# Order of the convolution's matmuls: by column shift instead of in two phases

## The chip, the cores and the metric

The kernel runs on one core of one Trainium2 chip. The metric is the device time of one execution in microseconds (us); the time of a kernel is the median over its runs. The core has five engines: TensorE (PE, the matmuls; its weight loads are shown apart as PEld), VectorE (DVE), ScalarE (ACT), GpSimd (POOL) and SyncE (SP, which here issues all the DMAs). They wait for one another by semaphores.

## The reference

A vision tower over 128 images of 64x64 pixels. It has a first part, the tokenizer, and seven transformer and expert stages behind it. Only the tokenizer is touched. It embeds each pixel in 32 channels and puts it through four layers, each of which adds a spectral branch and a 3x3 convolution:

```
for i in range(nl):                                   # nl = 4, 32 channels
    h_ft = jnp.fft.rfft2(h)
    w_c = spec_wr[i] + 1j * spec_wi[i]
    out_modes = jnp.einsum('bixy,ioxy->boxy', h_ft[:, :, :mx, :my], w_c)
    spec = jnp.fft.irfft2(out_modes, s=(H, W))
    conv = lax.conv_general_dilated(h, conv_w[i], (1, 1), 'SAME', dimension_numbers=dn)
    conv = conv + conv_b[i][None, :, None, None]
    h = leaky(spec + conv)
```

## The kernel before

Everything is float32. The images are handled in 64 pairs. A pair fills the 128 partitions of a tile `rows_in` as four sections of 32 channels: image a (0 or 1) times s, where s says whether the row of pixels is even or odd. A section holds 32 rows of 64 columns, 2048 pixels, which are cut into four parts p of 512 pixels.

The convolution of the first layer works on the three input channels (`pe_x_conv`, L587) and is not touched. In the other three layers (the loop over `l`, 1 and 2, called mid, and the last one) each pair runs `pe_conv`, so it runs 3 x 64 = 192 times. Its result lies in four PSUM banks, `zbank` 0 to 3, bank 2a + s for image a and output rows of parity s, and part p in the 32 partitions from 32p. A 3x3 convolution needs for each output row its own row and the two beside it, at three column shifts dx:

- an output row of either parity takes two of its three rows from one row index of the input: an even row of the pair and the odd row beside it. Both stand in 64 partitions, so that one matmul with 64 rows and 32 columns of the array does both ("same-row taps", L612). The array holds eight such tiles at a time: two images a by four parts p. There are 3 dx x 2 parities x 8 = 48 such matmuls.
- the third row comes from the row index above or below, in 32 partitions ("neighbour-row taps", L619). The array holds sixteen such 32x32 tiles: 4 sections by 4 parts. There are 3 x 16 = 48 of these.

The profile shows each of these matmuls as two records, the second half of the float32 product behind the first. I call the records of one set of tiles that run at the same time a pass: 8 records for same-row taps, 16 for neighbour-row taps. Before, a pair has 12 passes of the first sort (phase one), then 6 of the second (phase two).

The program of TensorE for pair n is written out in `pe_pair`: `pe_conv` of pair n; then, for the pair before, the transposes `pe_flip` (L631) and the forward transform `pe_forward` (L648), and between them the inverse transform `pe_inverse` of the next pair (L568). At the end of the convolution the semaphore `z_done` lets VectorE add bias and spectral part (L966) and apply the leaky slope (L973); SyncE loads the rows of a later pair behind it (L351). In the last layer the flips and forward transforms are replaced by two small products `pe_q1` (L677) and `pe_q2` (L688).

Inside `pe_conv` there is one semaphore wait that matters here: `gb`, where `pe_forward` collects its result, is `zbank` 3. ScalarE copies it out (`modes_copy`, L841) and then raises `g_ready`. Output rows of odd parity (`so == 1`) go to banks 1 and 3, so TensorE waits for `g_ready` before the first of them in the mid layers.

The loop of a mid layer has two pairs in its body (`over_layer`, L204).

Of the kernel before, what the change touches and what calls it, by code (L numbers as in the profile page):

```python
# [28 lines left out]
ET = 2 + XT  # L29
# [35 lines left out]
def build_tokenizer(nc, x_pairs, grid_rows, embed_w, embed_b, spec_uv, conv_w, conv_b, q1_w, q1_b, q2_w, q2_b,  # L65
                    fwd_dram, inv_dram, sign_dram, eye_dram, tok, h_dram, g_dram, m_dram):

    with ExitStack() as ctx:
# [95 lines left out]
        g_ready = sem("g_ready")  # L164
# [25 lines left out]
        def pe_need(pe, signal, value):  # L190

            if not (isinstance(value, int) and value <= 0):
                pe.wait_ge(signal, value)
                pe.nop(nofuse=True)
# [396 lines left out]
        def pe_conv(pe, u, i, kind, l):  # L591

            n = 2 * i + u + PAIRS * l
            pe_need(pe, z_free, 2 * n)
            pe.wait_ge(rows_loaded[u], 32 * (i + NP * (l - 1) + 1))
            pe.nop(nofuse=True)
            SHIFTED = ((1, slice(0, COLS), slice(0, COLS)), (0, slice(1, COLS), slice(0, COLS - 1)),
                       (2, slice(0, COLS - 1), slice(1, COLS)))

            def moving(part, p, down, cols):  # L600
                start = COLS * (1 + down)
                return rows_in[u][part, start:start + PIX].rearrange("c (h q j w) -> c q h j w", h=2, q=4, w=COLS)[:, p, :, :, cols]

            for so in range(2):
                if so == 1 and kind != "last":
                    pe.wait_ge(g_ready, ET + n - 1)
                    pe.nop(nofuse=True)
                for dx, out, src in SHIFTED:
                    for p in range(4):
                        for a in range(2):  # L610
                            part = slice(64 * a, 64 * a + 64)
                            nc.tensor.matmul(section(zb[32 * p:32 * p + 32, 2 * a + so, :])[:, :, :, out],  # L612
                                             conv_t[part, dx, so, :], moving(part, p, 0, src), start=(dx == 1), stop=False)
            for dx, out, src in SHIFTED:
                for p in range(4):
                    for a in range(2):
                        for s in range(2):
                            part = slice(32 * (2 * a + s), 32 * (2 * a + s) + 32)
                            last = nc.tensor.matmul(section(zb[32 * p:32 * p + 32, 2 * a + 1 - s, :])[:, :, :, out],  # L619
                                                    conv_t[part, dx, 2, :], moving(part, p, -1 if s else 1, src),  # L620
                                                    start=False, stop=(dx == 2))
            last.then_inc(z_done, 1)
# [68 lines left out]
        def pe_pair(pe, u, i, kind, l):  # L691
# [10 lines left out]
            if kind == "first":  # L702
                pe_x_conv(pe, u, i, l)
            else:
                pe_conv(pe, u, i, kind, l)
# [619 lines left out]
class Signals:  # L1325
# [13 lines left out]
    def sem(self, stage, who):  # L1339
        return self.sems[stage, who]  # L1340
# [1638 lines left out]
```

## Time and profile before

| | |
|---|---|
| median of 3 runs | 8086.82 us (8085.25 to 8110.36) |
| the profiled execution | 8098.54 us, span 8096.7 us |
| mean granted TensorE clock | 0.924 |
| busy share of the span | PE 84%, PEld 50%, DVE 61%, ACT 28%, POOL 1% |
| L612 matmul records | 18432, 1151.4 us busy |
| L619 matmul records | 18432, 653.8 us busy |

The span runs from the first to the last instruction of the profiled execution. A busy share is an average over stages with different limits. The ends of matmul records are modelled, so a row's start is better evidence than its end. A granted clock of 1.00 is TensorE's higher level of 2.4 GHz, 0.5 is 1.2 GHz.

### The profile page before, as it was taken

The numbers are of one execution on the slowest core, as the hardware profiler recorded it, in microseconds if no ns is written. First come the engines' busy times: TensorE is split into PE (matmuls) and PEld (weight loads), VectorE is DVE, ScalarE is ACT, GpSimd is POOL, SyncE is SP. The second block draws the span as 40 slices with busy tenths as digits, with TensorE's granted clock in tenths as the row PEclk, the third lists the DMA queues.
The fourth block names the chain that finished last, engine by engine and source line by source line (L and its number), as shares of the span: only waits on it lengthen the run. The fifth ranks groups of instructions, "written<-read, shape, count | busy, mean of one in ns | idle before, by whom it ended". The sixth has DMA issues, their size and how long they took to land. (4 is left out here: it accounts for less than half of the span.)

```text
span 8096.7 us, 285876 instructions
## 1 busy us (share of the span) xinstructions
PE 6837.6 (84%) x120694; PEld 4060.7 (50%) x120694; DVE 4950.5 (61%) x7875; ACT 2232.6 (28%) x3074; POOL 63.0 (1%) x46
## 2 busy tenths in 40 slices
PE   4699986989889699989878999966888888888888
PEld 3566665555555555555554444433344444444443
DVE  2599993666666376666636777756455454454554
ACT  1133321222222122222212222223333333333333
POOL 1000000000000000000000000000000000000000
PEclk7799997999999799999979999978999999999999
DMA  6677775444444544444452222220000000000000
GB/s 182 136 134 135 137 141 147 115 116 115 117 116 114 153 120 116 116 117 115 114 158 69 72 72 72 72 67 3 1 3 3 1 3 3 1 3 3 1 3 2
DMA packets 714748, 641.00 MB, mean 79 GB/s; under 512 B 334881, under 2 KB 583841, under 8 KB 705831
## 3 DMA queue, kind: packets, MB, share of 16 engines
q1 hardware_dynamic: 713800, 626.58, 31.8%
q8 instruction: 814, 13.34, 0.7%
q14 instruction: 134, 1.09, 0.0%
HBM read 353.72 MB, written 285.56 MB: 79 GB/s over the span
## 5 line engine op out<-in xcount | busy, mean ns | idle before, releaser
L612 PE MATMUL zbank<-rows_in,conv_taps 64*32 64x512 f32 (+1 forms) x18432 | 1151.4, 642 | 239.5 <-issue 239.5
L966 DVE SCALAR_TENSOR_TENSOR rows_out<-zbank,conv_bias,work 128x1024 f32<-128x1024 f32 x512 | 633.8, 1279 | 1159.8 <-PE zbank L619 1143.5
L568 PE MATMUL abank<-inv_basis,mode_tile 128*32 128x128 f32 x32768 | 1014.8, 276 | 91.6 <-DMA mode_tile<-m_img 54.9
L834 ACT ACTIVATE turned<-tbank 128x1024 f32<-128x1024 f32 x400 | 410.1, 1025 | 2260.3 <-PE tbank L631 2260.3
L568 PEld LDWEIGHTS abank<-inv_basis,mode_tile 128*32 128x32 f32 x32768 | 884.6, 111 | 255.2 <-issue 254.8
L648 PE MATMUL zbank<-fwd_basis,turned 128*32 128x128 f32 x24576 | 756.1, 274 | 106.2 <-DVE rows_out L966 68.7
L612 PEld LDWEIGHTS zbank<-rows_in,conv_taps 64*32 64x32 f32 x18432 | 381.6, 114 | 919.6 <-issue 905.2
L648 PEld LDWEIGHTS zbank<-fwd_basis,turned 128*32 128x32 f32 x24576 | 682.6, 111 | 128.6 <-issue 127.4
L619 PE MATMUL zbank<-rows_in,conv_taps 32*32 32x512 f32 (+1 forms) x18432 | 653.8, 595 | 6.1 <-issue 6.1
L973 DVE SCALAR_TENSOR_TENSOR rows_out<-rows_out 128x1024 f32<-128x1024 f32 x512 | 601.7, 1217 | 0.0
L1559 PE MATMUL banks<-constants 128*128 128x512 f32 x1040 | 520.8, 654 | 22.4 <-issue 22.4
L988 DVE TENSOR_TENSOR folded<-by_row 128x1024 f32<-128x1024 f32 x400 | 471.3, 1218 | 46.0 <-PE tbank L631 45.6
L619 PEld LDWEIGHTS zbank<-rows_in,conv_taps 32*32 32x32 f32 x18432 | 279.4, 103 | 365.3 <-issue 317.5
L631 PE MATMUL tbank<-eye,folded 128*128 128x128 f32 x3200 | 439.7, 281 | 23.4 <-DVE folded L988 23.4
L631 PEld LDWEIGHTS tbank<-eye,folded 128*128 128x128 f32 x3200 | 346.1, 141 | 220.7 <-issue 220.7
L942 DVE TENSOR_TENSOR work<-spectra 128x512 f32<-128x512 f32 x512 | 330.5, 687 | 78.1 <-ACT spectra L828 78.0
L942 DVE TENSOR_TENSOR work<-inv_copy 128x512 f32<-128x512 f32 x512 | 329.2, 684 | 69.3 <-ACT inv_copy L828 69.3
L828 ACT ACTIVATE inv_copy<-abank 128x1024 f32<-128x1024 f32 x256 | 262.2, 1024 | 342.5 <-PE abank L568 342.5
L1559 PEld LDWEIGHTS banks<-constants 128*128 128x128 f32 x1040 | 211.6, 212 | 262.0 <-issue 259.8
L828 ACT ACTIVATE spectra<-abank 128x1024 f32<-128x1024 f32 x256 | 262.5, 1025 | 260.5 <-PE abank L568 260.5
L1559 PE MATMUL banks<-xT_stacked,weights 64*128 64x512 f32 (+1 forms) x896 | 288.2, 681 | 44.3 <-ACT xT_stacked L1524 31.2
L951 DVE TENSOR_TENSOR work<-work 128x1024 f32<-128x1024 f32 x256 | 312.2, 1219 | 2.3
(356 smaller groups left out, 7672.5 us busy)
## 6 DMA issues: line engine op xcount, KB each, us to landing
h_rows<-rows_out SPq DMA_DIRECT2D x768, 256.0 KB, 3.8
rows_in<-h_rows SPq DMA_DIRECT2D x384, 512.0 KB, 4.9
m_img<-rows_out SPq DMA_DIRECT2D x32, 1024.0 KB, 5.4
mode_tile<-m_img SPq DMA_DIRECT2D x512, 64.0 KB, 3.0
g_half<-modes_out SPq DMA_DIRECT2D x384, 64.0 KB
spectra<-g_half SPq DMA_DIRECT2D x12, 1856.0 KB, 27.3
rows_in<-x_slots SPq DMA_DIRECT2D x96, 194.9 KB
rows_out<-x_slots SPq DMA_DIRECT2D x96, 194.9 KB
```

Of the source, the lines that this page charges most:

```text
L568: last = nc.tensor.matmul(ab[32 * p:32 * p + 32, s, 128 * k:128 * k + 128], mode_tile[u][:, k, a, :], inv[:, k, s, 128 * p:128 * p + 128], ...
L612: nc.tensor.matmul(section(zb[32 * p:32 * p + 32, 2 * a + so, :])[:, :, :, out], conv_t[part, dx, so, :], moving(part, p, 0, src), start=( ...
L619: last = nc.tensor.matmul(section(zb[32 * p:32 * p + 32, 2 * a + 1 - s, :])[:, :, :, out], conv_t[part, dx, 2, :], moving(part, p, -1 if s ...
L631: last = nc.tensor.transpose(tb[:, x, 128 * b:128 * b + 128], folded[:, q, x, b, :], eye[:])
L648: last = nc.tensor.matmul(by_mode(gb[at:at + 32, 0:256])[:, :, :, q, :], turned[q][:, x, 2 * a + s, 32 * p:32 * p + 32], fwd[:, p, 2 * x + ...
L828: nc.scalar.activation(inv_copy[a], ab[:], ACT.Identity).then_inc(a_copied, 1)
L834: nc.scalar.activation(turned[q][:].rearrange("p x b n -> p x (b n)"), tb[:], ACT.Identity)\
L942: last = nc.vector.tensor_tensor(inverse[:, :, 2 * a:2 * a + 2, h, :].rearrange("p y s m -> p s y m"), up, low, op)
L966: nc.vector.scalar_tensor_tensor(out=rows_out[u][:, half].rearrange("p (s x) -> p s x", s=2), in0=zb[:, 2 * a:2 * a + 2, :], scalar=conv_b ...
L973: nc.vector.scalar_tensor_tensor(out=out, in0=out, scalar=0.01, in1=out, op0=ALU.mult, op1=ALU.max)\
L988: nc.vector.tensor_tensor(folded[:, y, :, :, :].rearrange("p x b (j w) -> p (x b j) w", w=COLS // 2), v[:, :, 0, :], v[:, :, 1, :], op).th ...
L1559: return nc.tensor.matmul(out, lhsT, rhs, start=start, stop=stop)
```

## The change

`pe_conv` issues the same 96 matmuls with the same operands, in another order. Before: all same-row taps (parity 0 with its three shifts, then parity 1), then all neighbour-row taps. After: for each shift dx the 8 same-row matmuls of parity 0, the 8 of parity 1, then the 16 neighbour-row matmuls. The wait for `g_ready` stays ahead of the first matmul of parity 1, which now has 8 matmuls ahead of it instead of 24.

```diff
-            for so in range(2):
-                if so == 1 and kind != "last":
-                    pe.wait_ge(g_ready, ET + n - 1)
-                    pe.nop(nofuse=True)
-                for dx, out, src in SHIFTED:
+            for dx, out, src in SHIFTED:
+                for so in range(2):
+                    if so == 1 and dx == 1 and kind != "last":
+                        pe.wait_ge(g_ready, ET + n - 1)
+                        pe.nop(nofuse=True)
                     for p in range(4):
                         for a in range(2):
                             part = slice(64 * a, 64 * a + 64)
                             nc.tensor.matmul(section(zb[32 * p:32 * p + 32, 2 * a + so, :])[:, :, :, out],
                                              conv_t[part, dx, so, :], moving(part, p, 0, src), start=(dx == 1), stop=False)
-            for dx, out, src in SHIFTED:
                 for p in range(4):
                     for a in range(2):
                         for s in range(2):
```

The new file is a line shorter, so L619 of before is L618 of after, and what follows moves by one line too. On TensorE, in the loop body of a mid layer, the convolution of the first of the two pairs stood like this before; a row gives line, operation, output, inputs, output shape and how many alike follow one another, and 32x512 is the unshifted tap, 32x8x63 the two shifted ones:

```order
L595 ISA [waits z_added]
L612 MATMUL zbank<-rows_in,conv_taps 32x512 [waits rows_loaded0]
L612 MATMUL zbank<-rows_in,conv_taps 32x512 x7
L612 MATMUL zbank<-rows_in,conv_taps 32x8x63 x16
L606 REGISTER_ALU
L612 MATMUL zbank<-rows_in,conv_taps 32x512 [waits g_ready]
L612 MATMUL zbank<-rows_in,conv_taps 32x512 x7
L612 MATMUL zbank<-rows_in,conv_taps 32x8x63 x16
L619 MATMUL zbank<-rows_in,conv_taps 32x512 x16
L619 MATMUL zbank<-rows_in,conv_taps 32x8x63 x32
```

The same place of the same engine after the change:

```order
L595 ISA [waits z_added]
L612 MATMUL zbank<-rows_in,conv_taps 32x512 [waits rows_loaded0]
L612 MATMUL zbank<-rows_in,conv_taps 32x512 x7
L607 REGISTER_ALU
L612 MATMUL zbank<-rows_in,conv_taps 32x512 [waits g_ready]
L612 MATMUL zbank<-rows_in,conv_taps 32x512 x7
L618 MATMUL zbank<-rows_in,conv_taps 32x512 x16
L612 MATMUL zbank<-rows_in,conv_taps 32x8x63 x16
L618 MATMUL zbank<-rows_in,conv_taps 32x8x63 x16
L612 MATMUL zbank<-rows_in,conv_taps 32x8x63 x16
L618 MATMUL zbank<-rows_in,conv_taps 32x8x63 x16
```

The array changes between 64x32 and 32x32 tiles five times in a pair instead of once, and the wait for `g_ready` stands 16 matmuls earlier. In the loop body of the last layer, which has no such wait, the same engine stood before like this, behind the product L677 of the pair before:

```order
L612 MATMUL zbank<-rows_in,conv_taps 32x8x63 x16
L612 MATMUL zbank<-rows_in,conv_taps 32x512 x8
L612 MATMUL zbank<-rows_in,conv_taps 32x8x63 x16
L619 MATMUL zbank<-rows_in,conv_taps 32x512 x16
L619 MATMUL zbank<-rows_in,conv_taps 32x8x63 x32
```

And after:

```order
L612 MATMUL zbank<-rows_in,conv_taps 32x512 x15
L618 MATMUL zbank<-rows_in,conv_taps 32x512 x16
L612 MATMUL zbank<-rows_in,conv_taps 32x8x63 x16
L618 MATMUL zbank<-rows_in,conv_taps 32x8x63 x16
L612 MATMUL zbank<-rows_in,conv_taps 32x8x63 x16
L618 MATMUL zbank<-rows_in,conv_taps 32x8x63 x16
```

Here too only the order moved: 48 matmuls of each sort stand in either list. No other engine's program changes.

## Rows read from the trace of the kernel before

**Rows 1.** The page: busy time by engine, and its two groups for the convolution.

```profile
PE 6837.6 (84%) x120694; PEld 4060.7 (50%) x120694; DVE 4950.5 (61%) x7875; ACT 2232.6 (28%) x3074; POOL 63.0 (1%) x46
...
L612 PE MATMUL zbank<-rows_in,conv_taps 64*32 64x512 f32 (+1 forms) x18432 | 1151.4, 642 | 239.5 <-issue 239.5
...
L619 PE MATMUL zbank<-rows_in,conv_taps 32*32 32x512 f32 (+1 forms) x18432 | 653.8, 595 | 6.1 <-issue 6.1
```

**Rows 2.** TensorE's waits in layer 2 (2801 to 4090 us), and line 204's branches.

```profile
PE zbank L612 <- issue: 114.3, 29, 4.8
...
L204 PEldq COMPARE_BRANCH  x90: 76/3504/4955, 352.1 to 4086.7; - x90
```

**Rows 3.** The timeline in layer 1, TensorE's rows: start, length, instructions.

```profile
2517.19 1.09 PE L631 MATMUL tbank<-eye,folded 128*128 128x128 f32 x8
...
2526.50 5.33 PE L612 MATMUL zbank<-rows_in,conv_taps 64*32 64x512 f32 x96
...
2531.76 3.38 PE L619 MATMUL zbank<-rows_in,conv_taps 32*32 32x512 f32 x96
...
2535.07 1.09 PE L631 MATMUL tbank<-eye,folded 128*128 128x128 f32 x8
```

**Rows 4.** Windows: length, busy PE, PEld, DVE, ACT, POOL, clock, DMA.

```profile
2526.50:2531.76 5.26, 5.26 (x101) 1.72 (x97) 5.26 (x6) 0.38 (x1) 0.00 (x0) 1.00 0.44 99
2531.76:2535.07 3.31, 3.31 (x105) 1.45 (x97) 0.02 (x1) 0.00 (x0) 0.00 (x0) 1.00 0.93 205
...
2505.69:2513.88 8.19, 8.19 (x96) 2.99 (x96) 1.13 (x1) 0.00 (x0) 0.00 (x0) 0.64 0.63 141
```

**Rows 5.** Timeline, four narrow windows around changes of the tile size.

```profile
2526.17 0.40 PE L648 MATMUL zbank<-fwd_basis,turned 128*32 128x128 f32 x8
2526.50 0.66 PE L612 MATMUL zbank<-rows_in,conv_taps 64*32 64x512 f32 x8
...
2531.20 0.63 PE L612 MATMUL zbank<-rows_in,conv_taps 64*32 64x504 f32 x8
2531.76 0.77 PE L619 MATMUL zbank<-rows_in,conv_taps 32*32 32x512 f32 x16
...
2534.42 0.71 PE L619 MATMUL zbank<-rows_in,conv_taps 32*32 32x504 f32 x9
2535.07 0.33 PE L631 MATMUL tbank<-eye,folded 128*128 128x128 f32 x1
...
4817.55 0.66 PE L677 MATMUL tbank<-rows_out,q_taps 32*32 32x512 f32 x8
4818.15 0.66 PE L612 MATMUL zbank<-rows_in,conv_taps 64*32 64x512 f32 x8
```

**Rows 6.** Timeline, narrow windows: pairs of same-row passes, by their first record.

```profile
2526.95 1.06 PE L612 MATMUL zbank<-rows_in,conv_taps 64*32 64x512 f32 x16
...
2527.38 1.05 PE L612 MATMUL zbank<-rows_in,conv_taps 64*32 64x504 f32 x16
```

**Rows 7.** Timeline, narrow windows in phase two: neighbour-row passes, by their first record.

```profile
2531.76 1.20 PE L619 MATMUL zbank<-rows_in,conv_taps 32*32 32x512 f32 x32
...
2532.21 1.01 PE L619 MATMUL zbank<-rows_in,conv_taps 32*32 32x512 f32 x17
...
2532.83 1.26 PE L619 MATMUL zbank<-rows_in,conv_taps 32*32 32x504 f32 x32
```

**Rows 8.** The timeline, layer 1: the copy behind `g_ready` and the store it releases.

```profile
2526.79 0.38 ACT L841 ACTIVATE modes_out<-zbank 128x256 f32<-128x256 f32 x1 [0.87 <-PE zbank L648]
...
2527.35 0.62 SPq L382 DMA_DIRECT2D g_half<-modes_out  x1
```

**Rows 9.** The timeline in the last layer: from one convolution to the next.

```profile
4826.82 2.48 DVE L966 SCALAR_TENSOR_TENSOR rows_out<-zbank,conv_bias,work 128x1024 f32<-128x1024 f32 x2 [5.04 <-PE zbank L619]
...
4832.69 1.28 DVE L1037 SCALAR_TENSOR_TENSOR turned<-tbank,q_bias,by_row 128x1024 f32<-128x1024 f32 x1
...
4834.11 1.09 PE L677 MATMUL tbank<-rows_out,q_taps 32*32 32x512 f32 x16 [1.34 <-DVE turned L1037]
```

## The prediction

> **What bounds the kernel now.** I read the page's busy shares first: TensorE leads with 84%, and the two groups of the convolution hold 1151.4 and 653.8 us of it [rows 1]. A share does not say that the engine is the limit where the change sits, so I asked who TensorE waits for in a mid layer. In the whole of layer 2 its one wait of size is ahead of L612, 29 times and 114.3 us in all, for nothing that the profile shows [rows 2]. It comes at the back edge of the loop: the branch of line 204 on TensorE's queue has a median of 3504 ns [rows 2]. It comes once in two pairs, and the order of the matmuls does not touch it. Everywhere else in the mid layers TensorE runs without a pause: the period of an undisturbed pair is 2535.07 - 2517.19 = 17.88 us [rows 3], and each engine that waits there waits for it. So in the mid layers a microsecond more in `pe_conv` is a microsecond more of time.
>
> In the last layer TensorE does wait, 1.34 us a pair, for VectorE's L1037 [rows 9]. That is no slack for the convolution: VectorE's chain starts with L966, which itself waits 5.04 us for the end of the convolution, and runs through L1037 to the product L677, behind which the next convolution starts [rows 9]. The convolution and that chain lie end to end, and here too its length counts in full.
>
> What is left is how long one convolution takes: 5.26 us for phase one and 3.31 us for phase two, 8.57 us, at a clock of 1.00 [rows 4].
>
> **What passes and switches cost.** The work of a pass never changes, only what lies between passes. A same-row pass follows the one before after 0.43 us (2526.95 to 2527.38) [rows 6], and the first one behind a change of tile size after 0.45 (2526.50 to 2526.95) [rows 5, 6]. A neighbour-row pass behind the first takes as long, 0.45 (2531.76 to 2532.21) [rows 7].
>
> A change of tile size is dearer. Four of them are in the rows, from 128x32, 64x32, 32x32 to 128x128 and 32x32 to 64x32. In each the new size's first record starts 0.06 to 0.07 us before the modelled end of the old size's last record: 2526.57 against 2526.50, 2531.83 against 2531.76, 2535.13 against 2535.07, 4818.21 against 4818.15 [rows 5]. Within one size the next pass starts on the first tile while the last ones still run; across a change it waits for the last tile. So a switch costs the stagger of the old pass and about 0.1 us:
>
> - behind a same-row pass (8 tiles): 2531.76 - 2531.20 = 0.56 us instead of 0.43 [rows 5]
> - behind a neighbour-row pass (16 tiles, further apart): the second pass ends at 2531.76 + 1.20 = 2532.96, so the new size would start at 2532.89, 0.68 us behind 2532.21 [rows 7].
>
> The order before pays something too. Phase two changes its shift twice without changing its tile size. There the 17th record of the row that starts at 2532.21 is alone, and the pass proper starts at 2532.83: 0.62 us instead of 0.43, so 0.19 us are lost at each of the two places [rows 7]. The last pass of phase two is staggered more as well: the three pieces 0.45 + 0.62 + 0.45 + 0.62 + 0.44 leave 0.73 of the 3.31 us for it, where I take 0.68 after the change.
>
> **The sum.** One shift after the change: four same-row passes, 0.45 + 0.43 + 0.42 + 0.56 = 1.86 us, and two neighbour-row passes, 0.45 + 0.68 = 1.13 us; together 2.99. Three shifts are 8.97 us, against 8.57: **+0.40 us** a pair. By parts it is four more switches (two at 0.13, two at 0.25, each with some 0.03 of restart, together 0.88 us) less two lost starts in phase two (0.4) and a shorter last stagger (0.05), which gives 0.43. I take 0.40. It comes 192 times: **+77 us**.
>
> The wait for `g_ready`: it stood behind six passes, and now stands behind two, 0.45 + 0.43 = 0.88 us behind the start, at 2527.38 in the pair of the rows. ScalarE's copy ends at 2526.79 + 0.38 = 2527.17, and the store that waits for the same semaphore is issued at 2527.35, 0.18 us behind the copy's end [rows 8]. TensorE needs its weight load on top of that. So the wait is hidden, or up to 0.1 us late, in the one pair of two that does not follow the branch; behind the branch the copy is long done. Behind the waiting instruction the whole rest of the convolution is queued, and VectorE waits for that. 62 pairs by 0.05 are 3 us. Bounds: nothing, or 0.4 us (the copy itself) in each of 128 mid pairs, 51 us.
>
> Pairs behind the branch start at the lower clock: their phase one takes 8.19 us at a mean clock of 0.64 [rows 4]. I add nothing for them. The time at the lower clock is set by what came before it, and a microsecond that a switch wastes there holds only half as many passes; a switch itself may be dearer. I allow 0 to 0.3 us for these 62 pairs, 0 to 19 us, in the range.
>
> The profiled execution is 8098.54 us, so it would become 8098.5 + 77 + 3 = 8179 us. It stands 12 us above the median of 8086.8, which I carry over: **8167 us**, 1.0% slower.
>
> On the switch the Trainium skill has a rule: "TensorEngine Tiling (Array Packing)", section "Key Properties", says that changing the tiling mode drains the engine. The rows agree, with 0.13 and 0.25 us for a drain. "TensorE: Matmul & The Clock Gate", section "Single matmul latency", puts the fixed part of one matmul that overlaps nothing at 398 cycles of 2.4 GHz, 166 ns. An estimate by that page is 4 x 0.166 - 0.4 = 0.26 us a pair, 50 us in all and 8140 us; the sum above goes by the rows instead.
>
> **The rivals.**
> 1. *The lost start moves instead of going away* (12%). If the 0.19 us of phase two come from the sixteen-tile passes draining the supply of instructions, then two passes of a pair still start late after the change, by 0.2 us each. That is 0.40 + 0.40 = 0.80 us a pair, 154 us in all, 8244 us. It decides if a switch leaves the same instructions as late as a change of shift does. Against it: the product L677 is a sixteen-record neighbour to L612, and the switch behind it is clean [rows 5]. But that has 8 tiles, not 16.
> 2. *The wait for `g_ready` shows* (8%): up to 51 us more, 8215 us. It shows if the semaphore reaches TensorE later than 0.2 us behind the copy. For it: the margin is only 0.03 us against the store's issue. Against: only one pair in two is so tight.
> 3. *Switches from 32x32 to 64x32 are free, and it gets faster* (5%). If the same-row weights were loaded while the sixteen tiles still run, the two switches back would cost nothing: 2 x 0.16 - 0.4 - 0.05 = -0.13 us a pair, -25 us, 8062 us. The point is a switch back of under 0.07 us. Against it: the one such switch in the rows took 0.60 us from pass to pass, 0.17 more than within one size [rows 5].
> 4. *No difference* (9%): TensorE's extra 0.4 us is given back, by shorter branches (the instruction fetch behind line 204 has more time) or shorter stretches at the lower clock. 77 us over 62 branches would take 1.2 us off each of them.
>
> **How the numbers follow.** The sum as it stands has 66%; its own range is 8125 to 8200 us (0.2 to 0.6 us a pair). Rivals 1 and 2 are above it and 3 and 4 below. From 8110 to 8235 us about 2 in 10 is left out. A measurement tells some 0.3%, 24 us. Slower by more than that is the sum and the first two rivals, 0.86; within it 0.09; faster 0.05.
>
> **What would show it.** Right: L612 and L618 alternate three times in 8.9 to 9.0 us, the pair's period is 18.3 us, the last layer's 17.4; behind each last same-row record 0.5 us to the first neighbour-row one; no passes of a single record in L618. Wrong: a pause ahead of the fourth group of L612 records (rival 2), single records or passes over 0.6 us inside the shifts (rival 1), a step from L618 to L612 of 0.45 us (rival 3), a median of line 204's branch well under 3504 ns (rival 4).

## The result, and the profile after

The change made the kernel slower: 8203.81 us (median of 4 runs, 8193.6 to 8215.92) against 8098.59 us for the kernel before in the same comparison (4 runs, 8085.25 to 8118.6). The ratio is 1.0132, 95% interval 1.0109 to 1.0154, so 105 us. Forecast were 8167 us and 80 us more. The profiled execution of after has a span of 8214.1 us.

The page of the kernel after: busy time, and its groups for the convolution. They answer to [rows 1].

```profile
PE 6936.4 (84%) x120694; PEld 3885.3 (47%) x120694; DVE 4949.1 (60%) x7875; ACT 2232.9 (27%) x3074; POOL 63.0 (1%) x46
...
L612 PE MATMUL zbank<-rows_in,conv_taps 64*32 64x512 f32 (+1 forms) x18432 | 1229.5, 642 | 253.9 <-issue 253.9
...
L618 PE MATMUL zbank<-rows_in,conv_taps 32*32 32x512 f32 (+1 forms) x18432 | 711.8, 628 | 6.2 <-issue 6.1
```

The counts are the same, and the two groups are busy for 78 and 58 us more. The mean of L612 is 642 ns in both: there the overlap of the records became less, and the single one is not longer in the mean. The mean of the neighbour-row group rose from 595 to 628 ns, for another reason. In convolutions that run wholly at the clock of 1.00 it is 594 ns before and 595 after; in those that the lower clock touches it went from 599 to 680 ns, because the low stretch at their start now covers neighbour-row passes too. The windows of an undisturbed convolution in layer 1 show it; they answer to [rows 4] (length, busy PE, PEld, DVE, ACT, POOL, clock, DMA share, GB/s):

```profile
2507.93:2509.81 1.88, 1.88 (x36) 0.43 (x32) 1.88 (x4) 0.38 (x1) 0.00 (x0) 1.00 0.00 0
2509.81:2510.94 1.13, 1.13 (x40) 0.29 (x32) 1.13 (x3) 0.00 (x0) 0.00 (x0) 1.00 0.35 79
2510.94:2512.79 1.85, 1.85 (x37) 0.49 (x32) 1.85 (x3) 0.00 (x0) 0.00 (x0) 1.00 0.73 166
2512.79:2513.90 1.11, 1.11 (x40) 0.29 (x32) 0.43 (x1) 0.00 (x0) 0.00 (x0) 1.00 0.75 175
2513.90:2515.76 1.86, 1.86 (x38) 0.50 (x33) 0.00 (x0) 0.00 (x0) 0.00 (x0) 1.00 0.97 252
2515.76:2516.87 1.11, 1.11 (x40) 0.28 (x32) 0.00 (x0) 0.00 (x0) 0.00 (x0) 1.00 0.78 171
sum 8.94, PE 8.94 PEld 2.28 DVE 5.29 ACT 0.38 POOL 0.00; mean PE 1.49 PEld 0.38 DVE 0.88 ACT 0.06 POOL 0.00
```

Three rounds of four same-row passes (1.88, 1.85, 1.86; forecast 1.86) and two neighbour-row passes (1.13, 1.11, 1.11; forecast 1.13), in all 8.94 us against 5.26 + 3.31 = 8.57 [rows 4]. All of it at a clock of 1.00. The switch that before never had, from 32x32 to 64x32 inside the convolution, in a narrow window of the timeline of after:

```profile
2510.27 0.74 PE L618 MATMUL zbank<-rows_in,conv_taps 32*32 32x512 f32 x16
2510.94 0.65 PE L612 MATMUL zbank<-rows_in,conv_taps 64*32 64x504 f32 x8
```

2510.94 - 2510.27 = 0.67 us from pass to pass, where a pass within one tile size follows after 0.43 [rows 6]. The new size starts 0.07 us before the modelled end of the old one, as at each switch of before [rows 5].

The copy behind `g_ready` (the semaphore that frees bank 3), to compare with [rows 8]:

```profile
2507.93 1.52 PE L612 MATMUL zbank<-rows_in,conv_taps 64*32 64x512 f32 x24
...
2508.22 0.38 ACT L840 ACTIVATE modes_out<-zbank 128x256 f32<-128x256 f32 x1 [0.87 <-PE zbank L647]
...
2508.78 0.62 SPq L382 DMA_DIRECT2D g_half<-modes_out  x1
```

The third same-row pass, the first that needs the semaphore, starts in this trace at 2508.82, 0.89 us behind the first, and has no pause ahead of it. The wait stayed hidden.

In the last layer two things are different that the sum does not have. The product behind the convolution in the timeline of before, and then the timeline of after, to compare with [rows 9]:

```profile
4826.72 1.04 PE L688 MATMUL tbank<-turned,q_bd 128*4 128x512 f32 x8
```

```profile
5341.22 1.28 DVE L1036 SCALAR_TENSOR_TENSOR turned<-tbank,q_bias,by_row 128x1024 f32<-128x1024 f32 x1
...
5342.65 1.09 PE L676 MATMUL tbank<-rows_out,q_taps 32*32 32x512 f32 x16 [1.43 <-DVE turned L1036]
...
5352.60 1.04 PE L687 MATMUL tbank<-turned,q_bd 128*4 128x512 f32 x8
...
5352.81 1.28 DVE L965 SCALAR_TENSOR_TENSOR rows_out<-zbank,conv_bias,work 128x1024 f32<-128x1024 f32 x1 [5.52 <-PE zbank L618]
```

VectorE starts 0.21 us behind TensorE's next instruction (5352.60 to 5352.81). Before it was 0.10: that product, then L688, starts at 4826.72, and L966 at 4826.82 [rows 9]. TensorE waits 1.43 us for L1036 instead of 1.34, and the period of the last layer became 17.45 us from 16.99, 0.46 more, of which the convolution is 0.37.

And some convolutions of this layer run partly at the lower clock. Two windows of after, each one convolution:

```profile
4399.10:4409.63 10.53, 10.53 (x200) 2.81 (x195) 3.58 (x4) 1.12 (x1) 0.00 (x0) 0.84 0.10 16
4418.19:4427.13 8.94, 8.94 (x200) 2.35 (x193) 3.58 (x4) 1.12 (x1) 0.00 (x0) 1.00 0.10 16
```

I counted 14 such convolutions of 10.53 us in the 64 of the layer (before: one). Each costs 10.53 - 8.94 = 1.59 us. I call them slow convolutions below; they are single convolutions inside one execution.

### The profile page after: what moved, and what is told of

It reads as the page before. It is cut to its first block and busy times, and to the rows that moved or that the text cites. A ratio compares the mean times of both kernels' runs of the same rounds, so it can differ in the third digit from the quotient of the medians.

```text
span 8214.1 us, 285876 instructions
## 1 busy us (share of the span) xinstructions
PE 6936.4 (84%) x120694; PEld 3885.3 (47%) x120694; DVE 4949.1 (60%) x7875; ACT 2232.9 (27%) x3074; POOL 63.0 (1%) x46
## 5 line engine op out<-in xcount | busy, mean ns | idle before, releaser
L612 PE MATMUL zbank<-rows_in,conv_taps 64*32 64x512 f32 (+1 forms) x18432 | 1229.5, 642 | 253.9 <-issue 253.9
L647 PE MATMUL zbank<-fwd_basis,turned 128*32 128x128 f32 x24576 | 757.0, 274 | 101.8 <-DVE rows_out L965 71.4
L612 PEld LDWEIGHTS zbank<-rows_in,conv_taps 64*32 64x32 f32 x18432 | 317.1, 111 | 1023.2 <-issue 1023.2
L618 PE MATMUL zbank<-rows_in,conv_taps 32*32 32x512 f32 (+1 forms) x18432 | 711.8, 628 | 6.2 <-issue 6.1
L618 PEld LDWEIGHTS zbank<-rows_in,conv_taps 32*32 32x32 f32 x18432 | 163.3, 106 | 541.2 <-issue 541.1
```

The source lines that it names most:

```text
L647: last = nc.tensor.matmul(by_mode(gb[at:at + 32, 0:256])[:, :, :, q, :], turned[q][:, x, 2 * a + s, 32 * p:32 * p + 32], fwd[:, p, 2 * x + ...
```

## The experiments

All ratios are to the kernel before, with the 95% interval; "slow" counts the slow convolutions of the last layer in the profiled execution, and the period is that layer's median. A ratio rests on 3 to 12 executions of the run, the other columns on one profiled execution each.

| run | ratio | convolution, us | last period, us | slow |
|---|---|---|---|---|
| before | 1 | 8.57 | 16.99 | 1 |
| after | 1.0132 (1.0109 to 1.0154) | 8.94 | 17.45 | 14 |
| e1, three switches | 1.0093 (1.0079 to 1.0107) | 8.80 | 17.31 | 10 |
| e2, last layer only | 1.0054 (1.0039 to 1.0069) | 8.57, last 8.93 | 17.45 | 15 |
| e3, mid layers only | 1.0054 (1.0042 to 1.0067) | 8.94, last 8.57 | 16.99 | 1 |
| e4, longer period alone | 1.0034 (1.0021 to 1.0047) | 8.57, last 9.04 | 17.46 | 1 |
| e5, other tile order, before | 1.0013 (1.0000 to 1.0026) | 8.57 | 16.99 | 1 |
| e6, other tile order, after | 1.0141 (1.0120 to 1.0163) | 8.93 | 17.45 | 14 |
| e7, filler in the wait, after | 1.0108 (1.0087 to 1.0129) | 8.93 | 17.45 | 0 |
| e8, VectorE + 64 columns | 1.0002 (0.9991 to 1.0014) | 8.57 | 16.99 | 1 |
| e9, VectorE + 192 columns | 0.9992 (0.9981 to 1.0004) | 8.57 | 17.07 | 1 |
| e9, VectorE + 512 columns | 1.0059 (1.0038 to 1.0080) | 8.57 | 17.40 | 13 |
| e10, before unrolled | 0.9943 (0.9923 to 0.9964) | 8.57 | 16.99 | 1 |
| e11, after unrolled | 1.0070 (1.0048 to 1.0092) | 8.93 | 17.45 | 14 |

**Three switches instead of five.** The two loops of `pe_conv` run over groups of shifts:

```diff
+            for shifts in (SHIFTED[:2], SHIFTED[2:]):
+                for so in range(2):
+                    if so == 1 and shifts[0][0] == 1 and kind != "last":
+                        (wait for g_ready)
+                    for dx, out, src in shifts:
+                        same_row(dx, out, src, so)
+                for dx, out, src in shifts:
+                    last = next_row(dx, out, src)
```

> Order: shifts 1 and 0 together (8 same-row passes, 4 neighbour-row passes), then shift 2 alone: three changes between the two tile sizes in a pair instead of one (before) or five (after). Theory of the switches (each costs the stagger of the old pass plus about 0.1 us; a change of shift inside the neighbour-row passes costs 0.2): the convolution takes 8.8 us in undisturbed pairs, against 8.57 before and 8.94 after, so +0.2 us by 192, some +45 us. Rival, the cost lies in going by shift at all (each shift begins with other weights): 8.9 us or more. Rival, the wait for g_ready behind fewer matmuls costs the time: no more than 8.6 us here, because it again stands behind four passes.

The convolution takes 8.80 us, as the switches have it, with `g_ready` back behind four passes. Windows of this kernel: eight same-row passes, four neighbour-row passes, then four and two.

```profile
2535.96:2539.53 3.57, 3.57 (x69) 1.10 (x65) 3.57 (x5) 0.38 (x1) 0.00 (x0) 1.00 0.19 46
2539.53:2541.79 2.26, 2.26 (x72) 0.86 (x64) 1.72 (x2) 0.00 (x0) 0.00 (x0) 1.00 0.88 198
2541.79:2543.64 1.85, 1.85 (x37) 0.49 (x32) 0.00 (x0) 0.00 (x0) 0.00 (x0) 1.00 0.97 258
2543.64:2544.77 1.13, 1.13 (x41) 0.30 (x33) 0.00 (x0) 0.00 (x0) 0.00 (x0) 1.00 0.72 153
```

The last two rounds are those of after. The second, four neighbour-row passes with one change of shift, is 2.26 = 2 x 1.13 us: what a switch between its two halves would cost is what the lost start costs. The whole run is 75 us slower than before (64 to 87), not 45: the last layer again has a longer period than its convolution explains (0.32 against 0.23) and ten slow convolutions. With 44 us for the switches, 6 and 15 us for these make 65, at the lower end of the interval.

**Where the rest lies: one layer at a time.** `pe_conv` takes the new order for one `kind` and the old one for the others:

```diff
+            if kind == "last":      # e3: if kind != "last":
+                (the loops of after)
+            else:
+                (the loops of before)
```

> The new order in the last layer alone (64 of 192 convolutions). Of the 105 us of the change, the switches there account for 64 by 0.37 = 24 us. The trace of after shows 13 convolutions of 10.53 us in the last layer where the granted clock fell to its lower level, before had 1. Theory that these belong to the last layer's new period: they are here too, 24 + 19 + 6 (a later start of VectorE) = 49 us, faster than after by 55. Rival, they are chance or come from the mid layers: 24 to 30 us.

> The new order in the two mid layers alone (128 of 192 convolutions). Theory of the switches: 128 by 0.37 to 0.43 = 47 to 55 us, the last layer's period is 16.99 us and one or two of its convolutions are at the lower clock. Rival, the 25 us that the sum lacks lie in the mid layers (branches, clock, g_ready): 75 us or more.

Each is 44 us slower than before (0.0054 of 8095; 32 to 56 and 34 to 54). The mid layers pay 128 x 0.37 = 47 us and no more. The last layer pays the same 44 us with half as many convolutions: 24 us of switches, and 20 more, with all its slow convolutions. Together they are 88 of the 105 us of after, whose own interval is 88 to 125. The forecast failed in the last layer, not in the mid ones.

**The period without the switches.** The order of before, and in the last layer eight more same-row matmuls ahead, whose result is overwritten:

```diff
+            if kind == "last":
+                for p in range(4):
+                    for a in range(2):
+                        part = slice(64 * a, 64 * a + 64)
+                        nc.tensor.matmul(section(zb[32 * p:32 * p + 32, 2 * a, :])[:, :, :, 0:35],
+                                         conv_t[part, 1, 0, :], moving(part, p, 0, slice(0, 35)), start=True, stop=True)
```

> The order of before everywhere. In the last layer alone each convolution starts with 8 more same-row matmuls of 280 columns, whose result the next ones overwrite: no further change of tile size, but a period of 16.99 + 0.47 = 17.45 us, as in after. Theory that the falls of the clock in the last layer come with the period and not with the switches: some 12 more convolutions at the lower clock, 30 + 19 = 49 us slower than before. Rival, the pauses of the switches are what lowers the clock: none more, 30 us slower.

The period is 17.46 us, as in after, and there is one slow convolution. The time is 28 us more (17 to 38), the 30 of the added matmuls. My theory of the period fell. But its rival as written does not follow either: in this kernel TensorE's wait ahead of L677 (here L683) is still 1.34 us, so two things of after are missing, the pauses inside the convolution and the longer wait. The next runs take them apart. Who waited for whom from 4400 to 5300 us, in us, times and the longest one, first in e4, then in after:

```profile
PE tbank L683 <- DVE turned L1043: 69.8, 52, 1.3
...
PE tbank L676 <- DVE turned L1036: 72.4, 50, 1.5
```

**The filler.** The order of after; in the last layer eight matmuls of 512 columns, whose result nobody reads, in the wait (the call alone is shown, not the function):

```diff
                 next_inverse(1)
                 if late:
+                    pe_filler(pe, n + 1 + layers)
                     pe_q1(pe, 1 - u, n - 1, 1)
```

> The order of after, and in the last layer eight more same-row matmuls of 512 columns, whose result nobody reads, in the 1.4 us for which TensorE waits ahead of the second L676. They need 0.9 us and should fit in. Theory that the clock falls at the start of a convolution because TensorE idled there for 1.44 us instead of 1.34 (VectorE starts 0.1 us later behind the new order): one slow convolution instead of 14 in the last layer, some 20 us faster than after. Rival, that the pauses inside the convolution are what lowers the clock: still 10 or more slow convolutions, no gain.

No slow convolution is left, at an unchanged period of 17.45 us and with all the pauses of the switches. The timeline of this kernel:

```profile
5352.51 1.09 PE L688 MATMUL zbank<-fwd_basis,conv_taps 64*32 64x512 f32 x16
5354.01 1.09 PE L676 MATMUL tbank<-rows_out,q_taps 32*32 32x512 f32 x16 [0.42 <-DVE turned L1046]
```

The wait is 0.42 us instead of 1.43. From the first convolution of the last layer to the end of the last one are 1105.1 us in this trace and 1128.3 in that of after, 23 us less. In whole runs the gain is 0.0024 of 8093, 19 us, which the two intervals do not separate; that the 14 slow convolutions cost some 22 us (14 x 1.59) is shown by the traces alone.

**A later VectorE, without the switches.** The order of before; in the last layer VectorE clears unused columns first:

```diff
                 dve.wait_ge(z_done, g + 1)
+                if kind == "last":
+                    nc.vector.memset(conv_bd[:, 0, :], 0.0)    # e9: conv_bd[:] (192 columns); folded[:, 0, 0, :, :] (512)
```

> The order of before. In the last layer VectorE clears 64 unused columns (0.1 us) ahead of L966, so that its chain ends 0.1 us later as after the change, and TensorE waits 1.44 us for L1037 instead of 1.34. Theory of the longer wait: slow convolutions appear in the last layer, ten or more, 6 + 16 = 22 us slower than before. Rival, pauses of the switches: one slow convolution, 6 us slower.

> As e8, whose 64 columns were hidden (TensorE's wait stayed 1.34 us): the order of before, and in the last layer VectorE clears 192 unused columns, 0.25 us, ahead of L966. It should lengthen TensorE's wait for L1037 to some 1.45 us, as after the change. Theory of the longer wait: ten or more slow convolutions in the last layer. Rival, something inside the new order's convolution lowers the clock: one slow convolution, period up by 0.1 us.

> The same with 512 columns, some 0.5 us: a wait of 1.7 to 1.8 us, more than after the change, and a period near its 17.45 us. Theory of the longer wait: slow convolutions in the last layer, as many as after the change or more. Rival: one.

The first was no test: the next instruction starts 0.03 us behind the clearing of the 64 columns, and the wait stayed at 1.35 us. With 192 columns the wait is 1.42 us and nothing happens; with 512 it is 1.76 us and 13 convolutions are slow, in a kernel without one switch more than before. The waits with 192 columns, as above, and the timeline with 512:

```profile
PE tbank L677 <- DVE turned L1039: 75.4, 53, 1.4
...
4818.17 1.09 PE L677 MATMUL tbank<-rows_out,q_taps 32*32 32x512 f32 x16 [1.76 <-DVE turned L1039]
4819.19 5.33 PE L612 MATMUL zbank<-rows_in,conv_taps 64*32 64x512 f32 x96
```

So a longer wait ahead of L677 brings slow convolutions without the new order, and the new order brings none without that wait (e7). Not settled is why 1.42 us in e9 brought none more and 1.43 in after 13 more: their periods differ too (17.07 and 17.45), and e4 has the period with a wait of 1.34 and one slow convolution, as before. That one is the third of the layer in all these kernels but e7, behind a single wait of 2.36 us or more.

The traces say one thing more. The others do not come at random. In after, from the sixth convolution on, every fourth or fifth is slow (they start 71.4 or 88.9 us apart); in e1, from the seventh on, every seventh (122.9 us); with 512 columns, from the fifth on, every fifth or sixth (88.7 or 106.1 us). So the period has a part in it beside the wait, and the 192 columns, at a period that no kernel with more slow convolutions has, are no clean test of a wait of 1.42 us.

**The order of the sixteen tiles.** Sections outside, parts p inside:

```diff
-                for p in range(4):
-                    for a in range(2):
-                        for s in range(2):
+                for a in range(2):
+                    for s in range(2):
+                        for p in range(4):
```

> The order of before in two phases, but within the 16 neighbour-row matmuls of a shift the sections are the outer loop and the parts p the inner one, so that neighbours in the program use the same 32 rows of the array and different columns. Tells what the 0.2 us are that before loses at each change of shift in phase two. Theory that the loss comes from weight loads that can be started ahead only where the array rows allow it: the pattern changes, the conv leaves 8.57 us, down to 8.15 if both losses go (-80 us), or up if more loads wait. Rival, that it comes from the supply of instructions in sixteen-tile passes whatever their order: 8.57 us and no difference.

> The same exchange of loops in the order of after. Here no shift changes inside a neighbour-row phase, so there is no lost start to win back. Theory: 8.94 us within 0.1, the same as after. Rival, the order of the sixteen tiles sets the stagger of a pass and so the price of each switch: 8.94 moves by three times the change of stagger.

No difference in either convolution; the ratio of the first, 1.0013, has an interval that just reaches 1. The passes of phase two with single records stand where they stood, with the same 0.19 us behind each. So the lost start does not hang on which tiles are neighbours in the program. What causes it stays open; the supply of instructions was the rival, and no run measured that.

**The branches.** TensorE's loop over a layer, unrolled once:

```diff
+            if eng is nc.tensor:
+                with eng.Fori(1, NP - 1, 2) as i:
+                    body(i)
+                    body(i + 1)
+            else:
+                (the loop of before)
```

> The order of before, with TensorE's loop over a mid layer unrolled once: four pairs in the body, 15 back edges a layer instead of 30. Each back edge costs 4.3 us of pause and some 2.1 us at the lower clock. Theory that the pause belongs to the branch: 30 fewer, some 190 us faster. Rival, that the instructions of a longer body must be fetched anyway and the pause comes as often: no difference.

> The same loop with the order of after. Theory that the change costs the same 0.37 us in a convolution whether it starts at the lower clock or not: slower than e10 by 100 us, as after is than before. Rival, that a good part of its cost lies in the pairs behind a back edge: nearer to 85 us.

The first is the fastest kernel of this study, 8047.5 us, by 46 us, not by 190. Its branch, and a pair of the first layer, from its trace:

```profile
L205 PEldq COMPARE_BRANCH  x45: 76/4071/6315, 381.1 to 4029.6; - x45
...
641.28 5.34 PE L592 MATMUL zbank<-rows_in,x_conv 128*32 128x512 f32 x32 [3.19 <-issue]
```

I had overlooked the first layer, which uses the same loop. Its 30 branches took 6.2 us in all before, 0.2 each; that is how a third of 90 branches lay far under the median of 3504 ns [rows 2]. With the longer body 15 take 59.6 us, 4.0 each, and the first convolution of layer 1 starts at 1447.4 us instead of 1340.0, 107 us later. In windows of the first layer TensorE's idle time grew by 74 us, 53 of them in the branches, and its busy time by 33 (862.8 us against 830.2), at a mean clock of 0.94 instead of 0.98. From the first to the last convolution the mid layers became 78 and 79 us shorter, some 5 us for each back edge that is gone. An estimate from that: unrolling the mid layers alone would give some 155 us; it was not run.

With the order of after the unrolled kernel is 98 us slower than e10 by the medians, as the theory has it (100, its rival 85). But the two profiled executions are 82 us apart, and in them the mid layers grew by only 13 and 15 us where 64 x 0.37 = 24 each were expected, so I leave this pair of runs open. The other traces answer the question better. In the seven runs with a body of two pairs and the old order in the mid layers, the convolutions behind a pause of the branch take 10.4 to 10.7 us in the mean; in the four with the order of after there, 11.0 to 11.1. That is about 0.4 us, as in the other pairs: the price of the order does not lie in the pairs behind a branch.

## Why the prediction was right, and where it was short

The direction was right, the time lies in the range (8110 to 8235), and the mechanism forecast as likeliest is the one that runs.

- *What bounds the kernel.* Right. TensorE has no slack in the mid layers, and e3's 44 us for 128 convolutions are their 0.37 us in full.
- *Passes and switches.* The mechanism was right, and the size to 0.03 us: 8.94 us for the convolution where 8.97 were forecast. A switch behind a neighbour-row pass, of which before had no example inside the convolution, took 0.67 us where 0.68 were read off a row of another place. e1 shows the same prices with another number of switches. The sum's term was 192 x 0.40 = 77 us; measured are 192 x 0.37 = 71.
- *The drain.* "TensorEngine Tiling (Array Packing)" of the Trainium skill, section "Key Properties", has changing the tiling mode drain the engine; the traces agree, with 0.56 and 0.67 us from pass to pass at a change of size in after where 0.43 is the rule. The prediction's estimate from the latency of a single matmul, 0.26 us a pair, fell short of the measured 0.37; the rows of before gave it better. A switch costs the stagger of the old pass, the time from its first record to its last (0.05 us for eight tiles, 0.16 for sixteen), and about 0.1 us, and the latency doesn't have the stagger.
- *`g_ready`.* Hidden, forecast at 3 us of 0 to 51.
- *Pairs behind the branch.* Nothing added beyond the 0.40, nearly right: their convolutions (58 behind a pause, where the prediction has 62) take 11.05 and 11.10 us in the mean of layers 1 and 2 where before took 10.66 and 10.63, 0.39 and 0.47 more. The trace of after has in 14 of them a pause of 0.1 to 0.9 us ahead of a neighbour-row pass, 6 us in all, for which the profile names no cause; in before there are two, 0.5 us in all, and in the other kernels with a body of two pairs and the old order two to seven (0.5 to 5 us). Three of the other four kernels with a body of two pairs and a new order there have 16 to 19 such pauses (6 to 7 us), the fourth, e6, 14 (3 us). In layer 2 of after:

```profile
PE zbank L618 <- issue: 2.5, 6, 0.8
```

- *The last layer.* Here the step failed. The prediction said that the convolution and VectorE's chain lie end to end and so its length counts in full, and took the chain as fixed. It became longer by 0.09 us because VectorE started later, 64 x 0.09 = 6 us, and the wait of TensorE with it, and the clock fell in 13 more convolutions, 13 x 1.59 = 21 us. These 27 us were not in the sum; the range had clock losses only for the mid layers.
- *The sum against the measurement.* 71 + 6 + 21 = 98, where 105 were measured, 88 to 125 by the interval; the two agree. In the traces the pauses at the branches were 6 us longer in after (in layer 2 29 of them are 119.9 us against 114.3 [rows 2]), but their mean runs from 3.8 to 4.1 us in the kernels of this study without a change there, so I take that as scatter. The rest of the miss, 12 us, was the level: carried to the first median of before, 8087, where four runs have 8099.
- *Rivals.* A lost start that moves (rival 1): no single record stands in L618. A wait that shows (rival 2): no pause at the third pass. Free switches (rival 3): 0.67 us against 0.43. Shorter branches (rival 4): the median of line 204 went from 3504 to 3707 ns, so nothing was given back.

## What to carry to other kernels

In these traces a matmul of another tile size started only 0.06 to 0.07 us before the modelled end of the last one of the old size, and the price could be read ahead of the change: the time from a pass's first record to its last, and about 0.1 us. Interleaving work of two tile sizes pays it at each change, so group by tile size unless the other order removes a wait of its own. And when a stage waits on a second engine, read the slack in that wait and the granted clock there too: 0.1 us more of waiting in each pair cost 6 us by itself, and 21 us more by what the clock did next.

## What was not expected of the hardware

- VectorE starts later behind the same last matmul when the last phase has only two passes: 0.71 to 0.72 us behind the start of that matmul's record in the median of after, e1, e6 and e7, and 0.62 in before, e3 (last layer), e4 and e5, while TensorE's next instruction follows after 0.51 us in all of them. The cause is open; the records' starts may not be those of the work where sixteen follow within 0.16 us.
- The granted clock fell during a convolution of the last layer in 14 of 64 otherwise equal pairs. In 13 of them TensorE had idled about 1.44 us ahead of L676 before it did. A filler of 0.9 us in that wait ended it.
- The back edge of the first layer's loop took 0.2 us in before and 4.0 us in e10, where its body is doubled.
